# Attention scores in halves: heads 0 and 1 wait for their own slot, and each half raises its own semaphore

## The chip, the cores and the metric

One Trainium2 chip, one core of it. The metric is the device time of one execution in microseconds (us), as the median of several runs.

## What is computed

A graph layer over 625 nodes with 256 features, in fp32 from and to memory. After a layer norm, three things are added up: a mean over the 20,000 edges' source rows (a linear layer on it and one on the node itself), a polynomial attention of 8 heads of 32 features, and the input. Then a second layer norm and a feed-forward of 8 experts with a hard choice of one expert per node. The change touches the attention alone, of which this is the core:

```python
y = A * jnp.einsum('bhni,bhnj,bhije->bhne', qn, qn, kv_mod) + scale ** 2 * Bc * jnp.einsum('bhnd,bhde->bhne', qn, kv) + scale ** 4 * Cc * vsum
y_norm, y = (y[..., :1], y[..., 1:])
y = y / y_norm
```

The quadratic term equals a sum over keys of (q·k + c)² times v, so the kernel computes scores, squares them, and multiplies the squares by v.

## The kernel before

The kernel is written engine by engine, with semaphores placed by hand; nothing schedules it. The stages follow one another: layer norm and projections; the matrix of edge counts by one-hot matmuls (lines 916 to 940), with small attention preparations between; the attention; transposes of the count matrix (line 1043); output projections and the second layer norm (lines 1051 to 1071); the hidden layer and its gate (lines 1081 to 1127); sorting of the rows by expert; the hidden layer again on sorted rows (lines 1102 to 1116); the experts (line 1186).

The attention has 20 squares: for two groups of four heads (`hg`), two halves of the 625 queries (`hf`, 313 and 312) and five tiles of 125 keys (`m`). The text calls one pass of `scores(u2)`, the two squarings and `values(u2)` **square u2**.

- `scores(u2)` (L1005 on PE): four matmuls, one per head, each with 32 rows of the array (`tile_position=(D * h, 0)`). Each leaves two MATMUL and two LDWEIGHTS records in the trace, so a square's scores are x8. Heads 0 and 1 go to one pair of PSUM banks and heads 2 and 3 to the next; such a pair is a slot, and there are `SLOTS = 3` of them in `ps` (banks 0 to 5).
- ACT (L527) takes one unit, which is one slot of two heads, per ACTIVATE: it adds a constant, squares, and writes `gsq` (in `qk_sb`, `NGB = 4` buffers). Two units make a square. The text calls them **a** (heads 0, 1) and **b** (heads 2, 3). Each raises `g_ready`.
- `values(u2)` (L1025 on PE): four matmuls of the squares with `v`, each into 32 columns of the array, accumulated over the five key tiles in bank 6 or 7. It waits for both units of its square and raises `g_used`.
- DVE (L738, L741) takes a finished half of queries out of bank 6 or 7 after the fifth `values` of it.

PE's order is written out: `scores(0)`, then `scores(u2 + 1)`, `values(u2)` for each u2. With three slots, `scores(u2 + 1)` needs the slot of square u2 - 1's b and that of square u2's a. The two waits on either side before the change:

```python
act.wait_ge(s_ps, u // 2 + 1)
if 2 * u2 + 2 > SLOTS:
    pe.wait_ge(g_ready, 2 * u2 + 2 - SLOTS)
```

After the last `values`, PE waits for all of `g_ready`, for the count matrix (`A_ready`) and for `y_left`, and transposes.

Of the kernel before, what the change touches and what calls it, by code (L numbers as in the profile page):

```python
# [19 lines left out]
def gps_layer(nc, x, edges, w_qkv, b_qk, b_v, w_lr, b_r, w_proj, b_proj, temp,  # L20
# [27 lines left out]
    with ExitStack() as ctx:  # L48
# [3 lines left out]
        def sem(name):  # L52
            return ctx.enter_context(nc.semaphore(name))
# [210 lines left out]
        s_ps = sem("s_ps")  # L264
        g_ready = sem("g_ready")
# [41 lines left out]
        def at_block(s, t):  # L307
            return ps[0:TP, s, TP * t:TP * (t + 1)] if t < 4 else ps[0:TP, 5 + s // 4, TP * (s % 4):TP * (s % 4 + 1)]
# [25 lines left out]
        def x_bank(j):  # L334
            return ps[:, 4 + j, :]
# [22 lines left out]
        SLOTS = 3  # L358
# [92 lines left out]
        def _(act):  # L451
# [68 lines left out]
            for u, (hg, hf, m, pr) in enumerate(units):  # L520
                lo, hi = HALF[hf]
                w = hi - lo
                act.wait_ge(s_ps, u // 2 + 1)
                if u >= NGB:
                    act.wait_ge(g_used, (u - NGB) // 2 + 1)
                b = 2 * (u % SLOTS)
                nc.scalar.activation(gsq[:, u % NGB, :, 0:w], ps[0:TP, b:b + 2, 0:w], ACT.Square,  # L527
                                     bias=sc2_col[0:TP, :]).then_inc(g_ready, 1)
# [324 lines left out]
        def _(pe):  # L853
# [8 lines left out]
            for j in range(3):  # L862
                first, last = 2 * j, min(2 * j + 2, T)
                pe.wait_ge(xn_ready, last)
                for c in range(KC):
                    for t in range(first, last):
                        at = TP * (c * (last - first) + t - first)
                        ins = nc.tensor.transpose(x_bank(j)[:, at:at + TP], xn[:, t, P * c:P * (c + 1)],
                                                  ident[0:TP, 0:TP])
# [117 lines left out]
            for b in range(7):  # L987
                ins = mm(ps[:, b, 0:2], zeros[:, 0:P], zeros[:, 0:2], start=False, stop=True, skip_group_check=True)
# [3 lines left out]
            def scores(u2):  # L992
                hg, hf, m, _ = units[2 * u2]
                lo, hi = HALF[hf]
                if u2 == 0:
                    pe.wait_ge(A_copied_a, 2)
                    pe.wait_ge(A_copied_v, 2)
                if u2 == 1:
                    pe.wait_ge(A_copied_a, 3)
                    pe.wait_ge(A_copied_v, 3)  # L1000
                if 2 * u2 + 2 > SLOTS:
                    pe.wait_ge(g_ready, 2 * u2 + 2 - SLOTS)
                for h in range(HG):
                    rows = slice(D * h, D * (h + 1))
                    ins = mm(ps[0:TP, 2 * ((2 * u2 + h // 2) % SLOTS) + h % 2, 0:hi - lo],  # L1005
                             kT[rows, hg, TP * m:TP * (m + 1)], qT[rows, hg, lo:hi], start=True, stop=True,
                             tile_position=(D * h, 0))
                ins.then_inc(s_ps, 1)


            def values(u2):
# [18 lines left out]

            U2 = len(units) // 2
            scores(0)
            for u2 in range(U2):
                if u2 + 1 < U2:
                    scores(u2 + 1)
                values(u2)
# [4 lines left out]
            for s in range(T):  # L1041
                for t in range(T):
                    ins = nc.tensor.transpose(at_block(s, t), A[:, t, TP * s:TP * (s + 1)], ident[0:TP, 0:TP])  # L1043
# [12 lines left out]
            for t in range(T):  # L1056
# [6 lines left out]
                for c in range(KC):  # L1063
                    ins = mm(ps[0:TP, b2, 0:C], yT[:, c, own], wproj_sb[:, c, :], start=False, stop=(c == KC - 1))  # L1064
# [5 lines left out]
                for s in range(T):  # L1070
                    ins = mm(ps[0:TP, b, 0:C], AT[:, s, own], z[:, s, :], start=(s == 0), stop=(s == T - 1))  # L1071
# [73 lines left out]
            for t in range(T):  # L1145
                pe.wait_ge(lgT_copied, 1 if t < 2 else 2)
                ins = mm(ps[0:TP, 6, E * t:E * (t + 1)], lgT[:, TP * t:TP * (t + 1)], part_sum[:, :],
                         start=True, stop=True)
# [10 lines left out]
            for c in range(KC):  # L1159
                for lo, hi in SPLIT:  # L1160
                    for n in range(3 * T):
                        if c == 0 and lo == 0 and n < T:
                            pe.wait_ge(perm_ready, n + 1)
                        ins = mm(psf[:, 1024 * c + lo:1024 * c + hi], xs[:, n // T, n % T, P * c:P * (c + 1)],  # L1164
                                 perm[:, n % T, lo:hi], start=(n == 0), stop=(n == 3 * T - 1))
# [13 lines left out]
            with pe.Fori(0, STEPS // EB) as i:  # L1179
                for b in range(EB):  # L1180
# [4 lines left out]
                    for k in range(KH):  # L1185
                        ins = mm(ps[0:TP, b, 0:C], hT_step[:, b, k, :],  # L1186
                                 wd_sb[:, bass.ds(e, 1), k, :], start=(k == 0), stop=(k == KH - 1))
# [48 lines left out]
```

## Time and profile before

| | |
|---|---|
| median of 3 runs | 286.92 us (286.75 to 287.32) |
| profiled execution, its own time | 286.28 us |
| its span (first to last instruction) | 284.5 us |
| granted TensorE clock, mean over the span | 0.972 of full |
| PE / ACT / DVE busy in the span | 246.6 / 156.2 / 140.4 us |
| ACT busy and idle at L527 (40 units) | 29.1 / 5.5 us |
| PE busy and idle at L1005 | 16.1 / 6.7 us |

Busy time of PE counts the time in which at least one matmul record is open; four matmuls on parts of the array overlap in it. A chain of waits follows the work that ended last, each step back to what released it. Idle time stands with the group before which it falls and with what ended it. The granted clock is the share of full speed that TensorE got in a stretch.

### The profile page before, as it was taken

How to read it: one execution, taken by the hardware profiler on the slowest of the kernel's cores; microseconds unless marked ns; L12 is line 12 of the kernel's file. 1: busy time of each engine (PE TensorE's matmuls, PEld its weight loads, DVE VectorE, ACT ScalarE, POOL GpSimd, SP SyncE). 2: the span in 40 equal slices, each digit the busy share in tenths (PEclk: the TensorE clock that was granted, in tenths of full speed). 3: DMA queues.
4: the chain of work that ended last, by engine and by line, in shares of the span. 5: the costliest groups of instructions: out<-in, count | busy, mean ns of one | idle time of the engine just before them, and what ended most of it. 6: DMA issues, size and time to landing. Idle time of an engine off the chain costs nothing.

```text
span 284.5 us, 4770 instructions
## 1 busy us (share of the span) xinstructions
PE 246.6 (87%) x1465; PEld 151.8 (53%) x1466; DVE 140.4 (49%) x396; ACT 156.2 (55%) x231; POOL 21.4 (8%) x40
## 2 busy tenths in 40 slices
PE   8699599988888887688879997699799989999990
PEld 3348267554444443222228884354345558888880
DVE  3997995995698960973003647700540013111110
ACT  3899540999999997888883011432204336222100
POOL 7000000000000000500000000000071000000331
PEclk9999867999999999999999999889999999999998
DMA  4650000000000000059930000000024000000011
GB/s 133 250 182 0 3 2 2 2 3 5 2 2 2 2 2 5 0 189 427 417 152 2 1 0 0 2 0 0 0 56 120 13 0 2 1 0 0 18 36 36
DMA packets 5912, 14.76 MB, mean 52 GB/s; under 512 B 2727, under 2 KB 3794, under 8 KB 4734
## 3 DMA queue, kind: packets, MB, share of 16 engines
q1 hardware_dynamic: 4462, 12.41, 11.8%
q0 software_dynamic: 1280, 1.31, 1.7%
q10 hardware_dynamic: 144, 0.66, 0.6%
q8 instruction: 20, 0.33, 0.5%
q14 instruction: 6, 0.05, 0.1%
HBM read 13.07 MB, written 1.30 MB: 51 GB/s over the span
## 4 chain that ended last, share of the span: by engine, by line
PE 54%; ACT 31%; DVE 10%; issue 2%; DMA 1%; POOL 0%; DVEq 0%; ACTq 0%
ACT mem L458 21%; PE ps L1186 15%; PE ps L1116 11%; PE ps L1005 6%; ACT qk_sb L527 6%; PE ps L1071 4%; PE ps L916 4%; PE ps L1164 3%; PE ps L1062 2%; PE ps L1064 2%; PE ps L1081 2%; DMA edges_sb<-in_edges 1%; PE ps L1043 1%; DVE mem L626 1%; PE ps L1127 1%
## 5 line engine op out<-in xcount | busy, mean ns | idle before, releaser
L458 ACT ACTIVATE mem<-ids_m,half_src 125x628 bf16<-125x628 f16 x109 | 79.1, 817 | 7.5 <-PE ps L940 4.4
L916 PE MATMUL ps<-mem 125*128 125x501 bf16 x160 | 50.8, 400 | 9.9 <-issue 4.9
L626 DVE TENSOR_SCALAR mem<-node_ids,dst_f 125x628 bf16<-125x628 f16 x160 | 51.2, 377 | 0.0
L1186 PE MATMUL ps<-mem 128*125 x192 | 41.7, 380 | 0.2 <-DVE row L836 0.2
L1186 PEld LDWEIGHTS ps<-mem 128*125 128x125 f32 x192 | 35.9, 188 | 5.9 <-issue 0.6
L918 PE MATMUL ps<-mem 125*128 125x126 bf16 x160 | 36.5, 228 | 0.0
L916 PEld LDWEIGHTS ps<-mem 125*128 x160 | 16.6, 104 | 30.5 <-issue 19.2
L1116 PE MATMUL ps<-xnT,w_sb 128*128 128x512 f32 (+1 forms) x104 | 30.6, 454 | 1.9 <-ACT mem L558 1.9
L527 ACT ACTIVATE qk_sb<-ps,sc_col 125x626 f32<-125x626 f32 (+1 forms) x40 | 29.1, 779 | 5.5 <-PE ps L1005 5.5
L1116 PEld LDWEIGHTS ps<-xnT,w_sb 128*128 128x128 f32 x104 | 16.8, 200 | 15.6 <-issue 13.5
L849 DVE SCALAR_TENSOR_TENSOR row<-ps,row 125x256 f32 x12 | 5.8, 485 | 36.6 <-PE ps L1186 36.6
L561 ACT ACTIVATE mem<-ps,b_sb 128x625 f32<-128x625 f32 x14 | 11.0, 782 | 22.1 <-PE ps L1116 21.8
L580 ACT COPY mem<-mem 128x1000 f32 x12 | 12.1, 1029 | 19.7 <-PE ps L1186 18.5
L1005 PE MATMUL ps<-mem 32*125 32x313 f32 (+1 forms) x160 | 16.1, 472 | 6.7 <-ACT qk_sb L527 5.3
L629 DVE TENSOR_SCALAR mem<-ids_m,src_f 125x628 bf16<-125x628 f16 x51 | 19.2, 377 | 0.0
L918 PEld LDWEIGHTS ps<-mem 125*128 x160 | 16.3, 102 | 2.0 <-issue 0.3
L1005 PEld LDWEIGHTS ps<-mem 32*125 32x125 f32 x160 | 6.2, 180 | 17.6 <-ACT qk_sb L527 14.7
L1025 PE MATMUL ps<-qk_sb,vz 125*32 125x313 f32 (+1 forms) x160 | 14.7, 439 | 0.9 <-ACT qk_sb L527 0.9
L875 PE MATMUL ps<-wqkv_sb,xnT 128*125 128x512 f32 (+1 forms) x40 | 14.1, 492 | 0.0
L441 POOL DMA_INDIRECT rows_sorted<-row,pos x5 | 6.2, 1233 | 90.8 <-DVE pos L810 89.5
L738 DVE SCALAR_TENSOR_TENSOR yT_sb<-ps,vs,mem 128x313 f32<-128x313 f32 (+1 forms) x4 | 2.2, 544 | 20.2 <-PE ps L1025 20.2
L1071 PE MATMUL ps<-vz,mem 125*125 125x256 f32 x50 | 11.6, 379 | 0.0
(198 smaller groups left out, 272.6 us busy)
## 6 DMA issues: line engine op xcount, KB each, us to landing
mem<-in_wd SPq DMA_DIRECT2D x8, 1024.0 KB, 13.2
w_sb<-in_w SPq DMA_DIRECT2D x1, 1024.0 KB, 8.8
wqkv_sb<-in_w_qkv SPq DMA_DIRECT2D x1, 768.0 KB, 4.2
x_all<-in_x ACTq DMA_DIRECT2D x1, 640.0 KB, 4.6
row<-rows_sorted SPq DMA_DIRECT2D x1, 579.7 KB
wlr_sb<-in_w_lr SPq DMA_DIRECT2D x1, 512.0 KB, 6.0
bqk_all<-in_b_qk SPq DMA_DIRECT2D x1, 256.0 KB, 5.1
wproj_sb<-in_w_proj SPq DMA_DIRECT2D x1, 256.0 KB, 6.6
```

What stands on the lines that cost most here:

```text
L458: ins = nc.scalar.activation(oh[:, g % OHB, 0, j, :], ids_m1[:, :], ACT.Sign, bias=half_src[:, g * GC + j:g * GC + j + 1])
L527: nc.scalar.activation(gsq[:, u % NGB, :, 0:w], ps[0:TP, b:b + 2, 0:w], ACT.Square, bias=sc2_col[0:TP, :]).then_inc(g_ready, 1)
L626: ins = nc.vector.tensor_scalar(oh[:, g % OHB, 1, j, :], node_ids[:, :], dst_f[:, col:col + 1], None, ALU.is_equal)
L629: ins = nc.vector.tensor_scalar(oh[:, g % OHB, 0, j, :], ids_m1[:, :], src_f[:, col:col + 1], 2.0, ALU.is_ge, ALU.mult)
L875: ins = mm(ps[0:TP, QKV_BANKS[n % 4], lo:hi], xnT[:, c, TP * t:TP * (t + 1)], w[:, c, :], start=(c == 0), stop=(c == KC - 1))
L916: mm(psf[:, bass.ds(first * BANK, TW + 1)], node_of, oh[:, buf, 0, j, 0:TW + 1], start=False, stop=False, skip_group_check=True)
L918: mm(psf[:, bass.ds(first * P + 5 * BANK, AW)], node_of, oh[:, buf, 0, j, TW:N + 1], start=False, stop=False, skip_group_check=True)
L1005: ins = mm(ps[0:TP, 2 * ((2 * u2 + h // 2) % SLOTS) + h % 2, 0:hi - lo], kT[rows, hg, TP * m:TP * (m + 1)], qT[rows, hg, lo:hi], start=Tru ...
L1025: ins = mm(ps[D * h:D * (h + 1), 6 + k % 2, 0:hi - lo], v[:, m, P * hg + D * h:P * hg + D * (h + 1)], gsq[:, (2 * u2 + pr) % NGB, i, 0:hi ...
L1071: ins = mm(ps[0:TP, b, 0:C], AT[:, s, own], z[:, s, :], start=(s == 0), stop=(s == T - 1))
L1116: ins = mm(psf[:, at + lo:at + hi], w1_sb[:, c, P * k:P * (k + 1)], x2nT[:, c, lo:hi], start=(c == 0), stop=(c == KC - 1))
L1186: ins = mm(ps[0:TP, b, 0:C], hT_step[:, b, k, :], wd_sb[:, bass.ds(e, 1), k, :], start=(k == 0), stop=(k == KH - 1))
```

## The change

`scores` no longer waits once ahead of its four matmuls. It waits ahead of head 0 for the slot of heads 0 and 1, and ahead of head 2 for the slot of heads 2 and 3, each only where that slot was in use before. `s_ps` is raised twice in a square, after head 1 and after head 3, and ACT waits for its own unit's raise. Matmuls, their operands and their order stay.

```diff
@@ -520,7 +520,7 @@
             for u, (hg, hf, m, pr) in enumerate(units):
                 lo, hi = HALF[hf]
                 w = hi - lo
-                act.wait_ge(s_ps, u // 2 + 1)
+                act.wait_ge(s_ps, u + 1)
                 if u >= NGB:
                     act.wait_ge(g_used, (u - NGB) // 2 + 1)
                 b = 2 * (u % SLOTS)
@@ -998,14 +998,16 @@
                 if u2 == 1:
                     pe.wait_ge(A_copied_a, 3)
                     pe.wait_ge(A_copied_v, 3)
-                if 2 * u2 + 2 > SLOTS:
-                    pe.wait_ge(g_ready, 2 * u2 + 2 - SLOTS)
                 for h in range(HG):
+                    need = 2 * u2 + h // 2 + 1 - SLOTS
+                    if h % 2 == 0 and need > 0:
+                        pe.wait_ge(g_ready, need)
                     rows = slice(D * h, D * (h + 1))
                     ins = mm(ps[0:TP, 2 * ((2 * u2 + h // 2) % SLOTS) + h % 2, 0:hi - lo],
                              kT[rows, hg, TP * m:TP * (m + 1)], qT[rows, hg, lo:hi], start=True, stop=True,
                              tile_position=(D * h, 0))
-                ins.then_inc(s_ps, 1)
+                    if h % 2:
+                        ins.then_inc(s_ps, 1)
 
 
             def values(u2):
```

No instruction changes place; what changes is where waits stand. On PE from `scores(1)` on, before the change (`mem` holds `kT` and `qT`, `qk_sb` holds the squares):

```order
L1005 MATMUL ps<-mem 125x313 [waits g_ready,A_copied_v,A_copied_a]
L1005 MATMUL ps<-mem 125x313 x3
L1025 MATMUL ps<-qk_sb,vz 32x313 [waits A_copied_a,g_ready]
L1025 MATMUL ps<-qk_sb,vz 32x313 x3
L1005 MATMUL ps<-mem 125x313 [waits g_ready]
L1005 MATMUL ps<-mem 125x313 x3
L1025 MATMUL ps<-qk_sb,vz 32x313 [waits g_ready]
L1025 MATMUL ps<-qk_sb,vz 32x313 x3
```

and the same place with the change:

```order
L1006 MATMUL ps<-mem 125x313 [waits A_copied_v,A_copied_a]
L1006 MATMUL ps<-mem 125x313
L1006 MATMUL ps<-mem 125x313 [waits g_ready]
L1006 MATMUL ps<-mem 125x313
L1027 MATMUL ps<-qk_sb,vz 32x313 [waits A_copied_a,g_ready]
L1027 MATMUL ps<-qk_sb,vz 32x313 x3
L1006 MATMUL ps<-mem 125x313 [waits g_ready]
L1006 MATMUL ps<-mem 125x313
L1006 MATMUL ps<-mem 125x313 [waits g_ready]
L1006 MATMUL ps<-mem 125x313
L1027 MATMUL ps<-qk_sb,vz 32x313 [waits g_ready]
L1027 MATMUL ps<-qk_sb,vz 32x313 x3
```

The wait that stood ahead of four matmuls stands ahead of the last two; the first two have a wait of their own, for one unit less.

## Rows read from the trace of the kernel before

**Rows 1.** The page, its head and part 1: span, busy time of each engine.

```profile
span 284.5 us, 4770 instructions
PE 246.6 (87%) x1465; PEld 151.8 (53%) x1466; DVE 140.4 (49%) x396; ACT 156.2 (55%) x231; POOL 21.4 (8%) x40
```

**Rows 2.** The page, part 4: the chain that ended last, by line.

```profile
ACT mem L458 21%; PE ps L1186 15%; PE ps L1116 11%; PE ps L1005 6%; ACT qk_sb L527 6%; PE ps L1071 4%; PE ps L916 4%; PE ps L1164 3%; PE ps L1062 2%; PE ps L1064 2%; PE ps L1081 2%; DMA edges_sb<-in_edges 1%; PE ps L1043 1%; DVE mem L626 1%; PE ps L1127 1%
```

**Rows 3.** Who waited for whom, 114.5 to 150.3 us: total, times, longest.

```profile
DVE yT_sb L738 <- PE ps L1025: 20.2, 4, 7.5
ACT qk_sb L527 <- PE ps L1005: 5.5, 20, 0.6
PE ps L1005 <- ACT qk_sb L527: 5.3, 19, 1.0
```

**Rows 4.** The chain of waits, squares 1 to 3: start us, us, what.

```profile
118.05 0.85 PE ps L1005 x8
118.90 0.02 issue
118.92 0.79 ACT qk_sb L527
119.72 0.04 issue
119.76 0.85 PE ps L1005 x8
```

**Rows 5.** The timeline of squares 0 to 2: start us, us, engine, line, idle before.

```profile
114.53 0.34 PEld L1005 LDWEIGHTS ps<-mem 32*125 32x125 f32 x8 [1.51 <-ACT mem L518]
115.42 1.46 ACT L527 ACTIVATE qk_sb<-ps,sc_col 125x626 f32<-125x626 f32 x2 [0.57 <-PE ps L1005]
116.32 0.34 PEld L1005 LDWEIGHTS ps<-mem 32*125 32x125 f32 x8 [1.45 <-issue]
117.09 0.73 PE L1025 MATMUL ps<-qk_sb,vz 125*32 125x313 f32 x8
117.21 1.46 ACT L527 ACTIVATE qk_sb<-ps,sc_col 125x626 f32<-125x626 f32 x2 [0.34 <-PE ps L1005]
118.05 0.81 PE L1005 MATMUL ps<-mem 32*125 32x313 f32 x8 [0.23 <-ACT qk_sb L527]
118.79 0.73 PE L1025 MATMUL ps<-qk_sb,vz 125*32 125x313 f32 x8
```

**Rows 6.** L1005's matmuls and weight loads in short stretches of square 2.

```profile
118.00:118.10 0.10, 0.05 (x4) 0.05 (x4) 1.00 0.00 0
118.10:118.20 0.10, 0.10 (x4) 0.10 (x8) 1.00 0.00 0
118.20:118.35 0.15, 0.15 (x4) 0.15 (x8) 1.00 0.00 0
118.35:118.50 0.15, 0.15 (x8) 0.01 (x2) 1.00 0.00 0
```

**Rows 7.** The chain of waits through the last square and past it.

```profile
147.12 0.81 PE ps L1005 x8
...
148.67 0.78 ACT qk_sb L527
149.45 0.04 issue
149.49 0.73 PE ps L1025 x8
150.23 2.92 PE ps L1043 x25
```

**Rows 8.** The timeline of the last square.

```profile
147.99 1.45 ACT L527 ACTIVATE qk_sb<-ps,sc_col 125x624 f32<-125x624 f32 x2 [0.26 <-PE ps L1005]
149.49 0.16 PEld L1025 LDWEIGHTS ps<-qk_sb,vz 125*32 125x32 f32 x8 [1.49 <-ACT qk_sb L527]
150.16 2.80 PEld L1043 LDWEIGHTS ps<-ident,at_sb 125*125 125x125 f32 x25 [0.51 <-issue]
150.29 0.54 DVE L738 SCALAR_TENSOR_TENSOR yT_sb<-ps,vs,mem 128x312 f32<-128x312 f32 x1 [7.51 <-PE ps L1025]
```

**Rows 9.** Stretches: us, PE, PEld, DVE, ACT, POOL busy (count), granted clock, DMA share, GB/s.

```profile
180.00:182.00 2.00, 0.54 (x5) 0.35 (x4) 1.97 (x2) 1.82 (x2) 0.00 (x0) 1.00 0.03 8
182.00:184.00 2.00, 1.55 (x3) 0.82 (x4) 1.09 (x2) 1.22 (x4) 0.00 (x0) 0.84 0.00 0
184.00:186.00 2.00, 2.00 (x6) 1.15 (x5) 0.00 (x0) 0.00 (x0) 0.00 (x0) 0.50 0.00 0
186.00:188.00 2.00, 2.00 (x6) 0.94 (x5) 0.00 (x0) 0.78 (x1) 0.00 (x0) 0.81 0.00 0
```

## The prediction

> **What bounds the kernel now.** I read the page first. PE is the busiest engine at 246.6 of 284.5 us [rows 1], but a share over all stages says little of one stage. The chain of waits divides the end among lines: the scores L1005 and the squaring L527 hold 6% each [rows 2]. So some 34 us of the chain run through the attention, on PE and ACT in turn. Who waited for whom says the same: ACT waited 5.5 us for the scores in 20 places, PE 5.3 us for the squaring in 19 [rows 3]. Each engine waits for the other once in every square, which is a loop and not a full engine.
>
> The chain shows the loop [rows 4]. Scores start at 118.05, ACT's unit a starts at 118.92, the next scores at 119.76. That is 0.87 from scores to a, 0.84 from the start of a to the next scores, 1.71 us a square. 17 squares later the same pattern stands: 118.05 + 17 × 1.71 = 147.12, where the scores of square 19 start [rows 7]. (18 starts from 118.05 to 147.12, squares 2 to 19.) Unit b and `values` are not in the loop.
>
> The other intervals, from start to start:
> - Scores to `values` on PE: 118.79 − 118.05 = 0.74 [rows 5].
> - `values` to the next work on PE, nothing awaited: 150.16 − 149.49 = 0.67. This is seen once, behind the last `values`, where transposes follow [rows 8].
> - a to b on ACT: 148.67 − 147.99 = 0.68 [rows 7, 8].
> - b to `values` where b is what it waits for: 149.49 − 148.67 = 0.82 [rows 7].
>
> **The change, part by part.**
>
> *The head 0 wait.* `scores(u + 1)` of heads 0 and 1 now needs b of square u − 1. `values(u − 1)`, ahead of it on PE, already waits for that unit, so this wait is free: heads 0 and 1 start when `values(u − 1)` lets PE go. Today they start with the rest, when a of square u is done.
>
> *The head 2 wait.* Heads 2 and 3 still wait for a of square u, 0.84 behind a's start. Behind this wait on PE stands `values(u)`, which needs b of square u anyway; b is ready 0.68 + 0.82 = 1.50 after a's start, heads 2 and 3 let PE go at 0.84 + 0.74 = 1.58. `values(u)` therefore starts 1.58 after a, as now (120.50 from 118.92).
>
> *The s_ps waits.* a needs only the first half. b needs the second half, 0.87 after that half starts, and follows a by 0.68 in any case. So b would wait only if the second half started more than 0.68 behind the first; in the sum below it is 0.30 behind at most.
>
> *The loop that is left.* Scores (heads 0, 1) of square u → a of u: 0.87. a → heads 2, 3 of u + 1: 0.84. These → `values(u)`: 0.74. `values(u)` → heads 0, 1 of square u + 2: 0.67. The sum is 3.12 us for **two** squares, 1.56 a square against 1.71. The loops beside it are shorter: by b (0.87 + 0.68 + 0.82 + 0.67 = 3.04 for two), PE alone (0.74 + 0.67 = 1.41), ACT alone (2 × 0.68 = 1.36).
>
> *The beginning.* `scores(1)` now starts its first half behind `scores(0)`: 114.53 + 0.74 = 115.27 instead of 116.32 [rows 5]. Its a follows ACT's b of square 0: 115.42 + 1.36 = 116.78 instead of 117.21. Its second half and `values(0)` at 117.09 stay. Scores of square 2 follow at 117.09 + 0.67 = 117.76 instead of 118.05: 0.29 sooner.
>
> *The rest.* From square 2 each two squares take 3.12 instead of 3.42. Square 18 is 8 such pairs on, so its scores start 0.29 + 8 × 0.30 = 2.69 sooner: 145.41 − 2.69 = 142.72. Square 19's first half starts 1.41 later (144.13), its a at 145.00, its b at 145.68, its `values` at 146.50. Today that is 149.49. **The stage ends 3.0 us sooner.** PE then goes into the transposes of 2.92 us [rows 7], which cover DVE's last take of y as they do now (L738 begins 0.13 behind them [rows 8]). DVE's earlier takes waited up to 7.5 us for `values` [rows 3], so nothing else is late. All later stages hang on this chain, so I pass the 3.0 on whole.
>
> *What it costs.* No matmul is added. One wait on PE and one raise a square are. That more waits cost nothing is an assumption; the rows' steps of 0.02 and 0.04 [rows 4] already hold one of each, so a bound for 20 more of both is 0 to 20 × 0.06 = 1.2 us. I take 0 and keep the rest for the range. The Trainium skill (TensorE: Matmul & The Clock Gate, "The cost: per-tile semaphore tail") speaks against this change: each further increment in a group of tiled matmuls adds some 26 ns at its end, and one on the last suffices. By it, 20 × 0.026 = 0.5 us, the gain would be an estimated 2.5 instead of 3.0. No row here has two raises in one group.
>
> The unknown price is whether the two halves still run side by side. Now all four heads do: four matmuls open in the first 0.05 us, stay four for 0.3 us, and the four second records open between 118.35 and 118.50 [rows 6]. So four heads take the time of one. With the second half held back by 0 to 0.30 us (in every other square heads 2 and 3 come 0.3 behind; in the rest both are free at once), nothing shows the overlap. The ends are 0, if each head's rows of the array work for themselves, and 0.74, if the second half must follow the first. I take 0, since four heads with two records each already interleave. The 0.67 is also borrowed; the nearest other row is 0.73, the busy time of `values`, with which the sum is 3.18 for two and the gain about 2.5.
>
> *The clock.* It fell to half in 184 to 186 and in part on either side, after PE was busy 0.54 of 2 us [rows 9]. The stretches lost 0.32 + 1.00 + 0.38 = 1.7 us of full clock. All of this moves by 3 us; one such fall more or less is worth up to 1.7 us either way.
>
> **The rivals.**
> 1. *The halves stagger (slower).* Heads 2 and 3 don't open until heads 0 and 1 are in their second records, 118.05 to some 118.42, so 0.37 behind. PE's own loop is then 0.37 + 0.74 + 0.67 = 1.78 a square, 0.07 over now: 18 × 0.07 − 0.3 at the beginning = +0.9 us, **287.9**. In full sequence (0.74 behind) it is 2.15 a square: 18 × 0.44 − 0.3 = +7.6, 294.5. It decides from a stagger of 0.30, where 1.41 + 0.30 meets 1.71. For it: the raise and the wait now cut the group of four. Against it: the interleaving of rows 6. The Trainium skill (same page, "What overlaps and what doesn't") says matmuls start and end strictly in order, while weight loads overlap where row groups differ. Read strictly, a second half behind both records of the first would give this rival. Rows 6 let four first records open ahead of four second ones.
> 2. *Part of the gain.* `values` → scores takes more than 0.67, the waits cost their 1.2, or the halves lose some tenths: 1.60 to 1.68 a square, 0.7 to 2 us gained, **285.4**.
> 3. *No change.* The first half doesn't in fact start sooner, for one of PE's queue reasons that no row shows: PE sits idle 0.24 behind each `values`, and if that is a turn-round time the loop stays 1.71. **286.6** with the beginning's 0.3. Against it: the transposes follow with no such idle time, and the idle time ends 0.04 behind a each time [rows 4].
>
> **How the numbers follow.** The profiled execution took 286.28, so the same kernel changed would take 283.3; the median is 0.64 above it, 286.92 − 3.0 = **283.9**. About 0.2% (0.6 us) is what a measurement of this kernel can tell from no change. Chances: forecast 0.62, rival 2 0.17, rival 3 0.08, rival 1 0.13. Faster: 0.79, same 0.08, slower 0.13. The forecast's own range is 282.2 (a clock fall less) to 285.6 (one more). The range of 8 in 10 leaves out rival 1 and a few per cent at the bottom: 282.2 to 286.9.
>
> **What would show it.** Scores' start-to-start alternates, about 1.41 and 1.71, and a's idle time before L527 falls from 0.25 in each square to near 0 in every other one and 0.2 in the rest. `values` of the last square starts near 146.5, the transposes follow. In squares where heads 2 and 3 come 0.3 later, four first records open in two twos and PE's group of scores lasts about 0.3 longer. If instead `values` starts more than 0.8 behind the second half, the halves don't overlap and rival 1 holds. If ACT's wait before a stays at 0.25 everywhere, rival 3 does. The prediction is wrong, too, if the stage ends 3 us sooner and the end doesn't.

## The result, and the profile after

The changed kernel takes 284.4 us, the median of 10 runs (283.82 to 286.49), against 286.95 before (285.78 to 288.16, 10 runs). The ratio is 0.993, with a 95% interval of 0.9902 to 0.9957: faster by 0.7%. Medians here and below are taken over all runs of a kernel; ratios and intervals are the recorded ones over its fast runs alone (at most 1.5% above its fastest run) and are not quotients of these medians (0.991 here). The profiled execution took 284.47 us, with a span of 282.7 us where the one before had 284.5.

The page, its head, part 1 and the line of part 4 that answer to [rows 1, 2]. Lines behind the change stand two further down: L1027 is `values`, L1045 the transposes, L1188 the experts.

```profile
span 282.7 us, 4770 instructions
PE 249.6 (88%) x1465; PEld 155.6 (55%) x1466; DVE 140.6 (50%) x396; ACT 155.7 (55%) x231; POOL 21.4 (8%) x40
...
ACT mem L458 22%; PE ps L1188 15%; PE ps L1118 11%; PE ps L1006 6%; PE ps L1027 4%; PE ps L1073 4%; PE ps L916 3%; PE ps L1166 3%; PE ps L875 2%; DMA edges_sb<-in_edges 2%; PE ps L1064 2%; PE ps L1083 2%; PE ps L1066 2%; PE ps L1045 1%; PE ps L1129 1%
```

The squaring L527 held 6% of the chain before. It is gone from the line, and `values` (L1027) has come in with 4%. Who waited for whom, 114 to 148 us (total, times, longest), answers to [rows 3]:

```profile
DVE yT_sb L738 <- PE ps L1027: 16.6, 4, 6.8
ACT qk_sb L527 <- PE ps L1006: 2.5, 10, 0.5
```

ACT waits for scores in 10 places instead of 20, and 2.5 us instead of 5.5. The timeline of three squares (start us, us, engine, line, idle before) shows the pattern:

```profile
117.74 0.81 PE L1006 MATMUL ps<-mem 32*125 32x313 f32 x8
118.48 0.73 PE L1027 MATMUL ps<-qk_sb,vz 125*32 125x313 f32 x8
118.58 2.86 ACT L527 ACTIVATE qk_sb<-ps,sc_col 125x626 f32<-125x626 f32 x4 [0.26 <-PE ps L1006]
119.14 1.07 PE L1006 MATMUL ps<-mem 32*125 32x313 f32 x8
120.14 0.73 PE L1027 MATMUL ps<-qk_sb,vz 125*32 125x313 f32 x8
120.81 0.81 PE L1006 MATMUL ps<-mem 32*125 32x313 f32 x8
121.54 0.73 PE L1027 MATMUL ps<-qk_sb,vz 125*32 125x313 f32 x8
121.65 2.85 ACT L527 ACTIVATE qk_sb<-ps,sc_col 125x626 f32<-125x626 f32 x4 [0.21 <-PE ps L1006]
```

Scores start at 117.74, 119.14 and 120.81: steps of 1.40 and 1.67, or 3.07 for two squares where it was 3.42. ACT now runs four units on end (x4) and then waits 0.21. PE is never idle here: every step begins where the one before lets go. The loop still runs through ACT in every other square: heads 2 and 3 of the square at 119.14 open at 119.42, which is 0.84 behind ACT's unit a at 118.58. In that square at 119.14 the two halves lie apart. In short stretches of L1006 alone (us, PE busy and count, PEld busy and count, clock, DMA share, GB/s):

```profile
119.14:119.24 0.10, 0.10 (x2) 0.10 (x2) 1.00 0.00 0
119.24:119.40 0.16, 0.16 (x2) 0.16 (x4) 1.00 0.00 0
119.40:119.47 0.07, 0.07 (x4) 0.07 (x4) 1.00 0.00 0
119.47:119.60 0.13, 0.13 (x6) 0.13 (x4) 1.00 0.00 0
```

Two matmuls open at 119.14 (heads 0 and 1) and two more between 119.40 and 119.47 (heads 2 and 3). From 119.52 six records are open, since two more have started at 119.51. The records don't name their heads, but where four heads start together at full clock the second records open about 0.36 behind the first ones ([rows 6]), so the pair at 119.51 belongs to the pair at 119.14: the second records of heads 0 and 1 run beside the first of heads 2 and 3. The group of eight lasts 1.07 us instead of 0.81, which is just the 0.27 that the second half starts later. So the halves run side by side.

The end of the stage and of the kernel in the chain of waits (start us, us, what):

```profile
145.98 0.73 PE ps L1027 x8
146.72 2.92 PE ps L1045 x25
```

and the experts, first in this trace, then in the one before the change:

```profile
232.75 43.40 PE ps L1188 x192
```

```profile
236.26 41.72 PE ps L1186 x192
```

Against [rows 7], where the last `values` stood at 149.49 and the transposes at 150.23, the chain is 3.51 us ahead. The experts took 41.72 us in the trace of before, and they take 43.40 here. The granted clock says why. Stretches of the changed kernel, with the columns of [rows 9]:

```profile
180.00:184.00 4.00, 4.00 (x11) 1.98 (x10) 0.00 (x0) 0.78 (x1) 0.00 (x0) 0.71 0.00 0
...
230.00:234.00 4.00, 3.67 (x15) 2.82 (x16) 2.11 (x5) 2.80 (x4) 0.00 (x0) 0.94 0.00 0
234.00:238.00 4.00, 4.00 (x14) 3.19 (x13) 0.00 (x0) 1.14 (x2) 0.00 (x0) 0.63 0.02 4
```

and the last two in the kernel before:

```profile
230.00:234.00 4.00, 3.13 (x16) 1.88 (x15) 0.80 (x1) 1.56 (x2) 0.00 (x0) 1.00 0.00 0
234.00:238.00 4.00, 3.83 (x18) 3.00 (x17) 2.11 (x5) 3.18 (x4) 0.00 (x0) 1.00 0.00 0
```

TensorE's clock stood at its lower level (1.2 instead of 2.4 GHz) for part of 230 to 238 in the one trace and not in the other: 4 × 0.06 + 4 × 0.37 = 1.7 us of full clock. The stretch at 180 to 184 stands in both traces ([rows 9] have it at 182 to 188). The span's difference of 1.8 is thus: scores begin 0.13 later, the stage takes 3.64 less (114.56 to 150.16 before, 114.69 to 146.65 after, first scores to first transpose), the experts take 1.7 more.

### The profile page after: what moved, and what is told of

Read it like the earlier page. It is cut to its first block, busy times and chain, and to the rows that moved or that the text cites. A ratio compares the mean times of both kernels' runs of the same rounds, so it can differ in the third digit from the quotient of the medians.

```text
span 282.7 us, 4770 instructions
## 1 busy us (share of the span) xinstructions
PE 249.6 (88%) x1465; PEld 155.6 (55%) x1466; DVE 140.6 (50%) x396; ACT 155.7 (55%) x231; POOL 21.4 (8%) x40
## 4 chain that ended last, share of the span: by engine, by line
PE 61%; ACT 26%; DVE 7%; issue 2%; DMA 2%; POOL 0%; DVEq 0%; ACTq 0%
ACT mem L458 22%; PE ps L1188 15%; PE ps L1118 11%; PE ps L1006 6%; PE ps L1027 4%; PE ps L1073 4%; PE ps L916 3%; PE ps L1166 3%; PE ps L875 2%; DMA edges_sb<-in_edges 2%; PE ps L1064 2%; PE ps L1083 2%; PE ps L1066 2%; PE ps L1045 1%; PE ps L1129 1%
## 5 line engine op out<-in xcount | busy, mean ns | idle before, releaser
L916 PE MATMUL ps<-mem 125*128 125x501 bf16 x160 | 50.0, 395 | 9.8 <-issue 4.7
L1188 PE MATMUL ps<-mem 128*125 x192 | 43.4, 391 | 0.2 <-DVE row L836 0.2
L1188 PEld LDWEIGHTS ps<-mem 128*125 128x125 f32 x192 | 37.1, 194 | 6.5 <-issue 0.6
L527 ACT ACTIVATE qk_sb<-ps,sc_col 125x626 f32<-125x626 f32 (+1 forms) x40 | 28.5, 778 | 2.5 <-PE ps L1006 2.5
L1006 PE MATMUL ps<-mem 32*125 32x313 f32 (+1 forms) x160 | 19.1, 472 | 1.7 <-DVE mem L722 1.4
L875 PE MATMUL ps<-wqkv_sb,xnT 128*125 128x512 f32 (+1 forms) x40 | 15.5, 531 | 0.0
L1006 PEld LDWEIGHTS ps<-mem 32*125 32x125 f32 x160 | 8.9, 181 | 11.6 <-ACT qk_sb L527 5.3
L1027 PE MATMUL ps<-qk_sb,vz 125*32 125x313 f32 (+1 forms) x160 | 14.7, 439 | 0.6 <-ACT qk_sb L527 0.6
L875 PEld LDWEIGHTS ps<-wqkv_sb,xnT 128*125 128x125 f32 x40 | 8.0, 204 | 6.1 <-issue 5.5
```

Source lines behind the costliest of these rows:

```text
L875: ins = mm(ps[0:TP, QKV_BANKS[n % 4], lo:hi], xnT[:, c, TP * t:TP * (t + 1)], w[:, c, :], start=(c == 0), stop=(c == KC - 1))
L916: mm(psf[:, bass.ds(first * BANK, TW + 1)], node_of, oh[:, buf, 0, j, 0:TW + 1], start=False, stop=False, skip_group_check=True)
L1027: ins = mm(ps[D * h:D * (h + 1), 6 + k % 2, 0:hi - lo], v[:, m, P * hg + D * h:P * hg + D * (h + 1)], gsq[:, (2 * u2 + pr) % NGB, i, 0:hi ...
L1188: ins = mm(ps[0:TP, b, 0:C], hT_step[:, b, k, :], wd_sb[:, bass.ds(e, 1), k, :], start=(k == 0), stop=(k == KH - 1))
```

## The experiments

The theory is a loop of four steps, with the lengths that the trace of the change shows: first half to unit a 0.84, a to second half 0.83, second half to `values` 0.72 where it opens late, `values` to the next first half 0.67. That is 3.06 for two squares. (The expectations below go by 0.85, 0.83, 0.74 and 0.66, whose sum of 3.08 is 0.02 too long.) What was open: whether both parts of the change are needed, whether the steps predict a kernel not yet seen, and where a third of the 3.6 us of the stage went.

**The waits alone.** On top of the change:

```diff
-                act.wait_ge(s_ps, u + 1)
+                act.wait_ge(s_ps, u // 2 + 1)
...
-                    if h % 2:
+                    if h == HG - 1:
                         ins.then_inc(s_ps, 1)
```

> The two waits on PE are split as in the change, but s_ps is raised once, behind head 3, and both of ACT's units wait for that. Theory (a loop of four steps): unit a then needs heads 2 and 3, which start 0.84 behind a of the square before, so the loop is 0.84 + 0.87 = 1.71 us a square as before the change. The stage lasts 35.0 us from the first scores to the last values, as before (the change: 31.3), and the time is 286.9, the same as before within 0.2%. Rival (the early start of heads 0 and 1 alone is worth part of the gain, since four heads then share less of the array at a time): 1.6 us a square, 285 us.

Measured: 285.74 us, ratio 0.9943 (0.9908 to 0.9977). Its trace has half clock early in the attention, so only squares behind that are compared. The timeline of two of them:

```profile
131.62 1.08 PE L1006 MATMUL ps<-mem 32*125 32x313 f32 x8
...
132.75 1.46 ACT L527 ACTIVATE qk_sb<-ps,sc_col 125x626 f32<-125x626 f32 x2 [0.22 <-PE ps L1006]
...
133.29 1.08 PE L1006 MATMUL ps<-mem 32*125 32x313 f32 x8
```

A square takes 1.67 us, not 1.71. Unit a starts 1.13 behind the first half. In this trace heads 2 and 3 open at 131.91, so a starts 0.84 behind them, and the next second half (133.58) 0.83 behind a. The theory's loop is right in shape, and the early first half gives little by itself. The theory missed 0.04 a square, some 0.7 us in all: 0.03 of it from scores to a (0.87 before the change), 0.01 from a to scores. The time lies between the theory's 286.9 and the rival's 285, nearer the rival; the square is nearer the theory's 1.71 than the rival's 1.6.

**The raises alone.** On top of the kernel before:

```diff
-                act.wait_ge(s_ps, u // 2 + 1)
+                act.wait_ge(s_ps, u + 1)
...
-                ins.then_inc(s_ps, 1)
+                    if h % 2:
+                        ins.then_inc(s_ps, 1)
```

> One wait on PE ahead of all four heads as before the change, but s_ps is raised behind head 1 and behind head 3, and ACT's unit a waits for the first raise only. Theory: heads 0 and 1 end 0.014 us before head 3, so the loop is 1.70 instead of 1.71, at most 0.3 us in all: same as before, 286.7. It also prices a second raise in one group of four heads: by the Trainium skill's 26 ns for each further increment (TensorE: Matmul & The Clock Gate, The cost: per-tile semaphore tail) scores to a would be 0.87 + 0.03 and the stage up to 0.5 us longer, 287.4; by my assumption it is nothing. Rival (the raise alone is the gain): 284.4.

Measured: 285.82 us, ratio 0.9923 (0.988 to 0.9967). The timeline:

```profile
132.69 0.31 PEld L1005 LDWEIGHTS ps<-mem 32*125 32x125 f32 x8 [0.78 <-ACT qk_sb L527]
...
133.53 1.46 ACT L527 ACTIVATE qk_sb<-ps,sc_col 125x626 f32<-125x626 f32 x2 [0.22 <-PE ps L1005]
...
134.37 0.31 PEld L1005 LDWEIGHTS ps<-mem 32*125 32x125 f32 x8 [0.78 <-ACT qk_sb L527]
```

Scores to unit a is 0.84 instead of 0.87, a square 1.68. The raise behind head 1 reaches ACT 0.03 sooner, more than the 0.014 that I expected from the spacing of the heads. The second raise in the group costs nothing on the path: `values` starts 0.74 behind the scores (132.69 to 133.43), as before. The median lies 0.9 under the expected 286.7, where 20 × 0.03 = 0.6 us are explained; the rival's 284.4 is 1.4 further down. The 26 ns that the Trainium skill (TensorE: Matmul & The Clock Gate, "The cost: per-tile semaphore tail") names for each further increment would stand behind head 3, where unit b has 0.68 us to spare, so this run neither shows nor refutes it. Each part alone gives 0.03 to 0.04 a square; together they give 0.18 (1.71 to 1.53). The gain of the stage is in having both. This is read from the traces: by their times alone the two partial kernels and the change can't be told apart for certain, since the three intervals (0.9908 to 0.9977, 0.988 to 0.9967, and 0.987 to 0.9944 below) overlap.

**The change again, twice.**

> The change unedited, to see which part of its trace repeats. Theory: the attention takes 31.3 us from first scores to last values in each profile; what differs from run to run is where TensorE's granted clock stands at half, 3.4 us at a time and worth 1.7 us each. The first profile of the change has one such stretch at 233.4 to 236.8, in the expert stage, which the profile of before lacks. If that is chance, this profile may lack it and its span is 281 us instead of 282.7, and the mean clock over many runs is as before the change. Rival (the shift of the later stages by 3.5 us brings the fall at that place always): the stretch is there again and every run of the change has it.

Measured: 284.19 us, ratio 0.9907 (0.987 to 0.9944), on a chip where the kernel before takes 286.69. The profile (span 280.8) has half clock in the attention and at the experts:

```profile
114.00:120.00 6.00, 5.71 (x47) 1.66 (x44) 5.97 (x5) 4.26 (x7) 1.91 (x4) 0.72 0.00 0
...
230.00:234.00 4.00, 3.83 (x13) 2.82 (x12) 1.09 (x3) 3.21 (x4) 0.00 (x0) 0.70 0.02 4
```

The stage takes 33.50 us so, 1.5 more than at full clock. The experts take 43.40 again.

> The change, unedited, for a third trace. Theory: 31.96 us from first scores to first transpose as in its first profile, or 33.5 with half clock in it, as in its second; 282.3 to 285.5. No rival differs here; it counts where the half clock stands.

Measured: 282.51 us, with 33.52 for the stage and half clock at the same two places. The part of the expectations that put the stretch at the experts down to chance found no support: all three traces of the change have it there, and so have those of e4 and e5 below, which each add one edit to it.

**The kernel before again.**

> The kernel before, unedited, for a second trace. Theory: first scores to first transpose last 35.6 us again, unless half clock stands in it (then some 1.5 more), and where TensorE's clock stands at half later on is a matter of the run: this trace may have the stretch at the start of the expert stage that the first one of before lacks. Rival (before never has it, and the change always): no such stretch behind 236.

Measured: 287.08 us. The stage takes 36.80 with half clock in it. The experts have none, as in the first trace:

```profile
237.09 41.71 PE ps L1186 x192
```

So two traces of before lack the stretch and three of the change have it. But the two partial kernels (e1, e2) have it too, and their attention ends less than a microsecond from where it ends before the change (150.00 and 150.78 against 150.16), so the later stages' shift by 3.5 us doesn't bring the stretch, as the rival in the expectation for e3 had it. The mean clock over many runs differs little: 0.9704 in 35 runs of before, 0.9695 in 22 of the change (10 and 12). One more stretch in every run would be 0.006. What the first two traces suggest, that the change always brings one more, is thus not borne out by the runs. What they do show is that the change gains less than 3.64 even at an equal mean clock. At 0.978 to 0.980 it takes 282.4 us (mean of 4 runs) where the kernel before takes 285.7 (12 runs), at 0.972 to 0.974 283.9 (4) and 286.4 (15), at 0.967 to 0.969 284.8 (13) and 287.7 (23): 3.2, 2.5 and 2.9 us. (At 0.961 to 0.963 it is 286.5 and 287.3, but with a single run of the change.) So it is not how often the clock falls; where it falls is what is left, and that is argued, not shown.

**A wait made later.** This asks the steps for a kernel that was not measured:

```diff
-                    need = 2 * u2 + h // 2 + 1 - SLOTS
-                    if h % 2 == 0 and need > 0:
+                    need = 2 * u2 + h + 1 - SLOTS
+                    if h % 2 == 0 and need > 0 and u2 > 0:
```

(For `u2 = 0` neither form waits, so the added condition changes nothing.)

> The change with one wait made later: heads 2 and 3 of the next scores wait for unit b of the square instead of unit a, so they start 1.50 us behind a instead of 0.83. Nothing else is edited. Theory, with the steps that the change's trace shows (a to b 0.68, b to second half 0.82, second half to values 0.74, values to next first half 0.66, first half to a 0.85): the loop is 3.75 us for two squares, against 3.06 in the change, and the attention ends 9 x 0.69 = 6.2 us later; 290.5. Rival (values waits for b anyway, so a second half that starts with b costs only what PE has too much, 0.1 a square): 286.5.

Measured: 292.25 us in two runs, ratio 1.018 (1.0124 to 1.0235). The timeline behind the disturbed first squares:

```profile
131.12 1.42 PE L1006 MATMUL ps<-mem 32*125 32x312 f32 x8
...
133.13 1.13 PE L1006 MATMUL ps<-mem 32*125 32x312 f32 x8
...
134.85 1.42 PE L1006 MATMUL ps<-mem 32*125 32x313 f32 x8
```

134.85 − 131.12 = 3.73 for two squares; the sum of steps said 3.75. The time missed 290.5 by 1.8. In this trace half clock held from 115.5 to 125.7, and a square took about 2.75 meanwhile, so the stage (41.90, first scores to first transpose) is 3.7 us longer than the 31.96 + 6.2 of the sum; the first scores start 1.8 sooner than in the change's first trace (112.90 against 114.69), which gives half of that back. The rival's 286.5 is out. The trace also bears out how the records pair up: with the halves 0.62 apart, they open two at a time at 131.12, 131.49, 131.74 and 132.11, each pair's second records 0.37 behind its first.

**Zeros into PE's idle places.** First one place (three matmuls of 512 columns into bank 7, ahead of the wait for the last Gelu):

> The change plus three matmuls of zeros into the free bank 7, on PE behind the last scores of the hidden layer, where it is idle 0.87 us before line 1175. They add work and leave none out. Theory: PE's thin stretch before the expert stage (0.87 us idle, then 2.4 us of matmuls with 8 rows) is what is followed by half clock at 233.4; with the idle part filled the fall goes or gets rarer, and the time is up to 1.7 us less than the change, 282.7 to 284.4. If the 8-row matmuls alone suffice for it, or the fall is set by something else, nothing changes: 284.4. If the zeros delay the next matmuls, 284.6.

Measured: 283.86 us, ratio to before 0.9904 (0.9872 to 0.9937), which is the change's own 0.9907: nothing. Half clock at the experts stays in its trace. Then three places:

```diff
+            pe.wait_ge(b7_free, JOBS)
+            busy_7(5)
             scores(0)
...
+                    if not again and k == 2:
+                        busy_7(8)
...
+            busy_7(3)
             pe.wait_ge(h_ready, 2 * KH)
             pe.wait_ge(selT_ready, 1)
```

> The change plus matmuls of zeros into bank 7 wherever PE sits idle ahead of a stretch that was seen at half clock: 5 before the first scores (idle 1.45 us while the banks are copied), 8 before the third block of the hidden layer (idle 1.9 us behind the table load), 3 before line 1175. Added work, nothing left out. Theory: the granted clock fell behind these idle stretches in 3, 5 and 5 of the 6 profiles; filled, it falls at the first two rarely or not, so the mean clock rises from 0.970 to 0.976 or more and the median falls by 1 to 2.5 us, to 282 to 283. Rival (the fills delay what they stand ahead of, or the falls are set elsewhere): 284.4 or more.

Measured: 280.01 us, ratio 0.9746 (0.971 to 0.9782), mean clock 0.988 over its six runs. This is less time than both kernels take and 2 us under the expected 282 to 283. (The expectation also counts one place wrongly: behind the table load the clock fell in 4 of the 6 traces, not in 5.) Stretches:

```profile
114.00:120.00 6.00, 5.36 (x53) 2.17 (x52) 5.96 (x5) 5.20 (x10) 3.54 (x6) 1.00 0.00 0
180.00:184.00 4.00, 4.00 (x16) 2.22 (x15) 0.00 (x0) 1.38 (x2) 0.00 (x0) 1.00 0.00 0
184.00:188.00 4.00, 4.00 (x19) 2.15 (x21) 0.00 (x0) 1.24 (x3) 0.00 (x0) 1.00 0.00 0
...
234.00:238.00 4.00, 4.00 (x20) 3.47 (x20) 0.48 (x1) 1.03 (x1) 0.00 (x0) 1.00 0.00 0
```

All at full clock, the experts' included, where the same three matmuls did nothing in e4. The zeros at the first scores delay nothing: they end at 114.17, and the scores start 0.35 later, when the copy that they wait for is done. What made the experts' stretch go is open. It isn't the time at which the stage starts: the experts start at 230.91 here, without the stretch, and at 230.83 in e3, with it.

**The change priced at full clock.** The same fills on the kernel before, beside a repeat:

> The kernel before the change with the same three fills of zeros as in e7, on the same chip as e10, which is the change with them. Added work, nothing left out. Theory: the fills are worth as much here as on the change, so this kernel takes 283.6 us and e10 3.6 us less: with half clock out of the way, the difference of the two is the whole of what the attention stage saves, 35.6 against 31.96 us. Rival (something behind the attention gives 1 us back, whatever the clock does): the two differ by 2.5 us, this one 282.5.

> e7 once more, beside e9. Theory: 280.0 us, as in e7, mean clock 0.984 or more. Rival (e7's six runs fell well by chance): half clock at the start of the expert stage comes back in some of them, 281.5.

Measured: 284.31 us (ratio to before 0.9909, 0.9873 to 0.9944) and 279.99 us (0.9747, 0.9699 to 0.9794). Mean clocks are 0.984 and 0.982. The two differ by 4.3 us, where the stage alone gives 3.63 (35.60 and 31.97 in their traces). That is near what the theory has, but these medians scatter (the runs span 283.07 to 285.00, and 278.96 to 284.61; means over all runs instead of medians give 3.4), and by themselves they put the rival's 2.5 out only narrowly. The two traces settle it. First scores, transposes and experts in the chain of waits, e9:

```profile
113.76 0.84 PE ps L1005 x8
...
149.43 2.92 PE ps L1049 x25
...
233.79 41.71 PE ps L1195 x192
```

and e10:

```profile
115.04 0.81 PE ps L1006 x8
...
147.08 2.92 PE ps L1051 x25
...
231.44 41.71 PE ps L1197 x192
```

From the transposes to the experts both take 84.36 us, at the experts both take 41.71, and behind them both take about 6.5. So nothing behind the attention gives anything back. The first scores start at 113.76 in the one and at 115.04 in the other, ahead of all that the change touches; their starts vary from 112.9 to 115.0 over all traces, and that is part of the scatter of the times.

## Why the prediction was right

The forecast was 283.9 and the time is 284.4. The range held it. The mechanism, a loop of four steps over two squares, is what the traces show; that the time came out so near is in part luck, as two errors offset each other (*Passed on whole*). By its steps:

- *The loop before, 1.71:* as read. It is unchanged in e9 (first scores to transposes 35.60).
- *The head 0 wait is free:* right. First halves start where `values` lets go, with no idle time between (117.74, 120.81).
- *The loop that is left:* forecast 3.12 for two squares, measured 3.06 to 3.07. First half to a is 0.84 instead of 0.87, a to second half 0.83 instead of 0.84, second half to `values` 0.72 instead of 0.74. The borrowed `values` → scores (0.67) measures 0.66 to 0.67: transposes were a good stand-in.
- *The alternation:* forecast 1.41 and 1.71, measured 1.40 and 1.67.
- *Side by side:* taken at 0 for stagger, with no row for it. It is 0: 1.07 against 0.81, for a start 0.27 later. Rival 1 falls. So do rival 3, since PE's idle time behind `values` is gone, and rival 2 as it was put: a square takes 1.53 and not 1.60 to 1.68, although its 285.4 is only 1.0 from the time. The strict order that the Trainium skill states (TensorE: Matmul & The Clock Gate, "What overlaps and what doesn't"), read as rival 1 read it, does not hold for these two-record matmuls: second records of heads 0 and 1 open behind first records of heads 2 and 3 and run beside them.
- *What waits and raises cost:* taken at 0, and nothing shows above that. All steps of the loop measure at or under their forecast, with one wait and one raise more in each square.
- *The beginning:* the second half of `scores(1)` starts 1.66 behind the first scores (116.35 from 114.69) and no longer 1.79, where I had left it. So square 2 starts 3.05 behind them instead of 3.49, 0.44 sooner where the forecast had 0.29.
- *The stage:* forecast 3.0, measured 3.64. The small errors all go one way: eight pairs of squares at nearly 0.06, 0.15 at the beginning, and 0.04 in the last two squares.
- *Passed on whole:* this is the step that failed in the plain kernels. The medians differ by 2.5, not 3.64 (the ratio's interval makes it 1.2 to 2.8). In the two profiled executions the stage ends 3.5 sooner and the span only 1.8, which comes near the sign of being wrong that the prediction named last. The forecast was thus near for two errors that offset: stage 0.6 too small, passing-on 1.1 too large. The profile shows one place of the loss, the experts at half clock for 1.7 us. That this explains the medians is only argued, since mean clocks are nearly equal; a stretch costs more where PE is the bound (1.7 at the experts) than where it waits (1.5 in the attention of the change, 1.2 in that of the kernel before: 33.50 against 31.96, 36.80 against 35.60), so where it falls counts beside how often. The comparison at equal mean clock points the same way. The filled pair (e9, e10) shows that nothing in the program itself gives the gain back. Why the experts' stretch stands in all seven traces that have some part of the change and not all three fills, and in neither trace of the kernel before, stays open.
- *The clock's 1.7 either way:* right in size (1.7 measured at the experts). I took one such place into account; there are more, at the first scores and at the experts among them.

## What to carry to other kernels

Two engines that each wait for the other once a step form a loop; write its steps start to start and sum them. Where a wait covers a group of tiled matmuls, splitting both sides of the handshake, the wait ahead and the raise behind, took the loop from 1.71 us over one square to 3.06 over two; either side alone gave about a fifth of the gain in a square. Before a small gain is judged by medians, look at the granted clock of both kernels, and price the change once with the idle places of TensorE filled.

## What the runs showed of the hardware beyond that

- Filling 1.45 us of idle PE before the attention, 1.9 us behind the table load and 0.87 us before the experts with matmuls of zeros was worth 4.2 us on the changed kernel (284.2 to 280.0), more than the change itself, and 2.3 us on the one before. Which of the three fills did it was not separated, but for the last: alone it gave nothing. The granted clock rose from 0.970 to between 0.982 and 0.988.
- Half clock in the attention costs the change 1.5 us even though it is a loop of two engines: in e3 two squares then took up to 4.0 us instead of 3.07. In the kernel before, where PE has idle time in each square, it cost 1.2.
- A raise behind the second of four tiled heads reached ACT 0.03 us sooner than one behind the fourth (0.84 against 0.87 behind the start of the scores). Where only the last two heads start together (e1), the raise behind them comes 0.84 after their start too.
